# Front rows of two wide attention layers moved behind the attention steps, and another order and more gather places at the end of the last expert layer

## What is computed

```
x = x + tanh(g_xattn[n]) * xattn_n(layernorm(x), ctx_1024)
x = x + tanh(g_ffn[n])   * ffn_n(layernorm(x))
```

## Time and profile before

| | |
|---|---|
| median of 3 runs | 2029.77 us |
| the profiled execution | 2032.64 us, span 2030.8 us |
| PE busy | 1775.6 us, 87% of the span |
| DVE, ACT, POOL busy | 1259.3, 974.7, 528.6 us |
| granted PE clock, mean | 0.931 of full |

### The profile page before, as it was taken

One profiled execution on the slowest core, in us unless ns is written; L12 is line 12 of the kernel. 1 busy time (PEld: TensorE's weight loads), 2 busy tenths in 40 slices (PEclk: granted clock), 3 DMA queues, 4 the chain that ended last, 5 costly groups with the idle time before them and its releaser, 6 DMA issues. The chain is left out here.

```text
span 2030.8 us, 32563 instructions
## 1 busy us (share of the span) xinstructions
PE 1775.6 (87%) x11808; PEld 1449.2 (71%) x11808; DVE 1259.3 (62%) x2310; ACT 974.7 (48%) x1739; POOL 528.6 (26%) x492
## 2 busy tenths in 40 slices
PE   6998899967799995799999889989799799798886
PEld 4667799812577774799999467777477566588874
DVE  6886587536355454588887665556423688756643
ACT  4652467414686671377775243334433255416740
POOL 2221334244333232222220720000000144203333
PEclk9998899988899997699999989989799999899998
DMA  3003478310100000567674320000000100026742
GB/s 108 17 17 125 133 261 247 110 57 0 48 1 11 6 12 24 209 231 249 228 233 149 104 72 1 1 1 1 22 1 1 57 6 17 30 73 201 236 128 84
DMA packets 97140, 178.33 MB, mean 88 GB/s; under 512 B 25184, under 2 KB 61946, under 8 KB 95914
## 3 DMA queue, kind: packets, MB, share of 16 engines
q1 hardware_dynamic: 85496, 146.00, 21.5%
q0 software_dynamic: 11232, 30.69, 5.2%
q10 hardware_dynamic: 288, 0.00, 0.0%
HBM read 149.38 MB, written 27.26 MB: 87 GB/s over the span
## 5 line engine op out<-in xcount | busy, mean ns | idle before, releaser
L1667 POOL DMA_INDIRECT f_block_rows_home<-normed_x,f_token_of_sb x138 | 168.3, 1220 | 444.0 <-PE psum L1713 325.0
L1693 PE MATMUL psum<-f_block_h_sb,f_w1h_home 128*128 128x256 f32 x736 | 211.6, 287 | 30.2 <-DVE f_block_l_sb L1887 11.0
L1693 PE MATMUL psum<-f_block_l_sb,f_w1h_home 128*128 128x256 f32 x736 | 207.0, 281 | 0.0
L1693 PE MATMUL psum<-f_block_h_sb,f_w1l_home 128*128 128x256 f32 x736 | 207.0, 281 | 0.0
L2301 PE MATMUL psum<-a_xT_home,context_w 128*128 128x256 f32 x704 | 188.9, 415 | 13.8 <-PEq L122 9.7
L1703 PE MATMUL psum<-f_w2h_home,f_hidden_h_home 128*128 128x256 f32 x644 | 187.3, 291 | 1.9 <-DVE f_hidden_l_home L1887 1.0
L1703 PE MATMUL psum<-f_w2h_home,f_hidden_l_home 128*128 128x256 f32 x644 | 181.8, 282 | 0.0
L1703 PE MATMUL psum<-f_w2l_home,f_hidden_h_home 128*128 128x256 f32 x644 | 181.7, 282 | 0.0
L2301 PEld LDWEIGHTS psum<-a_xT_home,context_w 128*128 128x128 f32 x704 | 136.5, 204 | 47.5 <-issue 20.0
L1693 PEld LDWEIGHTS psum<-f_block_h_sb,f_w1h_home 128*128 128x128 f32 x736 | 141.2, 192 | 38.5 <-issue 28.6
L2466 ACT ACTIVATE a_probsT_sb<-psum 77x1024 f32<-77x1024 f32 (+1 forms) x128 | 130.6, 1020 | 74.8 <-PE psum L2353 72.1
(11 more groups left out here) (314 smaller groups left out, 3967.1 us busy)
## 6 DMA issues: line engine op xcount, KB each, us to landing
f_w_sb<-in_f_w SPq DMA_DIRECT2D x161, 512.0 KB
sorted_y<-f_result_sb SPq DMA_DIRECT2D x69, 256.0 KB
normed_x<-f_xn_all SPq DMA_DIRECT2D x24, 256.0 KB, 2.1
f_b_row_sb<-in_f_b SPq DMA_DIRECT2D x46, 128.0 KB
f_w_sb<-in_f_w SPq DMA_DIRECT2D x23, 256.0 KB
f_block_rows_home<-normed_x,f_token_of_sb POOLq DMA_INDIRECT x138
residual<-in_x SPq DMA_DIRECT2D x8, 256.0 KB, 6.3
context_w<-in_a_wk SPq DMA_DIRECT2D x2, 1024.0 KB, 5.1
```

Source lines behind the costliest of these rows:

```text
L1667: nc.gpsimd.indirect_dma_start(block_rows[b % 2][:, h, :], None, xs, bass.IndirectOffsetOnAxis(ap=column, axis=0)).then_inc(sems[f"rows_in ...
L1693: last = nc.tensor.matmul(hid_ps(q)[:, m, :], w, rhs, start=(j == 0), stop=(j == len(parts) - 1))
```

## The change

Three edits.

1. **Wide layers (1 and 2): the front comes behind.** With BEHIND = GROUPS + 2 = 34, `turn` of batch b is in step 34 + b, `route` in 35 + b, `logits_out` in 36 + b, and the steps go on to 43 (44 on DVE). In layer 1 the normalise of each batch stays where it was. In layer 2 that of batches 0 and 1 stays, and batch b = 2 ... 7 is normalised in step 32 + b. Layers 0 and 3 are as before.
2. **Layer 2, POOL:** all eight powers first, then all eight `add_row`. Before, they alternated.
3. **End of the last expert part:** 32 gather places (the other 16 in `xn_all`, which is free by then), so that no gather waits for a combine. DVE's order becomes: gates of units 0, 1, 2, shared result of the first batch, combines 0 to 2, gate 3, combines 3 to 6; gate 4, shared result, combines 7 to 10, gate 5, combines 11 to 14; gate 6, shared result, combines 15 to 18, gate 7, combines 19 to 22; shared result, combines 23 to 31.

In expert layer 0 the ring (8) and the order stay.

```diff
-    COMBINED = (1, 7) if shared == 1 else (4, 12, 20)
+    COMBINED = (1, 7) if shared == 1 else (3, 11, 19)
+    GATED_THEN = (7, 15, 23)
...
-    RING = 8 if own else 16
+    RING = 8 if own else 32 if t["last"] else 16
...
-    gathered = [w1[j // 4][:]... for j in range(RING)]
+    gathered = [w1[j // 4][:]... for j in range(min(RING, 16))]
+    gathered += [t["xn_all"][:, j, :] for j in range(RING - 16)]
...
-        combined = 0
+        combined, v0 = 0, U0 + BLOCKS * per_expert
+        if silu:
+            gated(dve, v0, v0 % 2)
+            gated(dve, v0 + 1, (v0 + 1) % 2)
         for k, b in enumerate(TAIL):
-            shared_block(b, U0 + BLOCKS * per_expert + k * shared)
+            more = silu and k + 1 < len(TAIL)
+            if more:
+                gated(dve, v0 + 2 * k + 2, (v0 + 2 * k + 2) % 2)
+            shared_result(dve, b, v0 + k * shared)
...
             combined = until
+            if more:
+                gated(dve, v0 + 2 * k + 3, (v0 + 2 * k + 3) % 2)
+                for j in range(combined, GATED_THEN[k]):
+                    combine(j)
+                combined = GATED_THEN[k]
...
-    FIRST, LAST = -Q_AHEAD, GROUPS + 6 + LAG
+    BEHIND = GROUPS + 2
+    FIRST, LAST = -Q_AHEAD, GROUPS + 6 + LAG if small else BEHIND + NBATCH + 2
+    XN_RING = None if FFN[n].get("routed") else 2
...
     def normed_at(s):
-        return output_at(s - 2 - LAG)
+        b = output_at(s - 2 - LAG)
+        if small or XN_RING is None:
+            return b
+        if b is not None and b < XN_RING:
+            return b
+        b = s - BEHIND + XN_RING
+        return b if XN_RING <= b < NBATCH else None
 
     def rows_at(s):
-        return output_at(s - 3 - LAG)
+        if small:
+            return output_at(s - 3)
+        return s - BEHIND if 0 <= s - BEHIND < NBATCH else None
 
     def logits_at(s):
-        return output_at(s - 4 - LAG)
+        if small:
+            return output_at(s - 4)
+        return rows_at(s - 1)
 
     def logits_out_at(s):
-        return output_at(s - 5 - LAG)
+        if small:
+            return output_at(s - 5)
+        return rows_at(s - 2)
...
                 for b in range(NBATCH):
                     front["power"](pool, b)
+                for b in range(NBATCH):
                     front["add_row"](pool, b)
```

More of the change, by code:

```diff
@@ L1517, in routed_experts @@
     result = [sb(f"result{s}", [P, BT, D]) for s in range(2)]
-    gathered = [w1[j // 4][:].rearrange("p c i -> p (c i)")[:, j % 4 * D:(j % 4 + 1) * D] for j in range(RING)]
+    gathered = [w1[j // 4][:].rearrange("p c i -> p (c i)")[:, j % 4 * D:(j % 4 + 1) * D] for j in range(min(RING, 16))]
+    gathered += [t["xn_all"][:, j, :] for j in range(RING - 16)]
     def rows_places(attention):
@@ L1879, in vector @@
     def vector(dve):
[L1880 to L1883, removed]
         def low(out, whole, part, sem):
```

## The result

The changed kernel takes 2011.95 us in the median of 4 runs (2007.16 to 2017.31), the kernel before 2029.71 beside it: ratio 0.9906, with 95% from 0.9879 to 0.9933. It is 17.8 us faster, half of the 35.5 that were forecast, and above the range's upper end of 2006. The profiled execution took 2017.31, 5.4 above the median (span 2015.5).

A forecast was written before the change was run, and what follows sets the result against it. PE was taken as the bound, losing time to waits for DVE's `logits_out`, half clock and reports held by gathers. Terms -42.5 - 15.5 + 12.5 + 5 + 5 = -35.5 took 2029.8 to 1994 us, range 1962 to 2006.

The forecast's parts named there:

- What bounds the kernel: Whole kernel: PE, busy 87%, loses time to waits for DVE's `logits_out`, half clock, and reports held back by gathers.
- Part 1: Steps of layer 2: without the front, batches lose its PE work, the waits and the half clock; 42.5 us less.
- Part 2: Steps of layer 1: batches fall from 32.1 to 28.9 us without the front; 15.5 us less in all.
- Part 3: Behind layer 2's last output: eight fronts in a row take 20 us instead of 7.4; cost 12.5 us.
- The circle: Behind layer 2's steps: `turn`, normalise, `logits_out` and `route` free one another in turn, 2.7 us a batch.
- Part 4: Behind layer 1's last output: routes held until the last batch's variance, then six follow; cost taken as 5 us.
- Part 5: End of the last layer: new order saves time, but 32 unbroken gathers delay PE's reports; 5 us more.
- the hold: Last expert part: a long unbroken row of gathers keeps PE's reports back until some 3.7 us behind its end.
- A: Rival, last layer's end: gathers don't delay PE's reports, so the end gains 23 us; 1966 us, chance 0.30.
- B: Rival, behind layers 1 and 2: fronts at half clock take 36 and 27 us; 2019 us, chance 0.06.
- C: Rival, steps of layers 1 and 2: PE's wait for the bank stays, so slower; 2047 us, chance 0.04.

The follow-up runs named there:

- rows_late: Changed kernel with POOL's `add_row` of batches 2 to 7 in layer 2 begun only when batch 5 is normalised: 2013.40 us (0.9914).
- best: Changed kernel with `logits_out` before normalise, six `add_row` late, layer 1's last variance behind four `logits_out`, POOL waiting for PE every fourth gather: 1978.64 us (0.9749).
- end_only: Kernel before with only the last layer's end changed (32 places, gates ahead of combines): 2039.68 us (1.0029).
- plain_halves: Changed kernel with 64 plain half-row transfers from POOL replacing the last layer's 32 gathers: 1974.55 us beside 2008.49; rerun 1970.01 beside 2009.4.
- last1: Changed kernel with `logits_out` before normalise in layers 1 and 2, and the last batch's variance and normalise later in layer 1: 1999.81 us (0.9848).
- after: First profile of the changed kernel itself: profiled execution 2017.31 us, where the median was 2011.95.
- again: Changed kernel itself, run again for a second profile: 2017.72 us (0.9925).

## Why the prediction was wrong, by its steps

**What bounds the kernel** was read rightly. With layer 2's front gone from the steps, wait and half clock are gone with it.

**Part 1** (-42.5): -41.7. Right, including its cycle of 26.0 us (26.2). (33.9 - 26.0 is 7.9 and not 7.8, and the three terms named for it add to 7.5; neither matters.)

**Part 2** (-15.5): -11.9 and -16.4 in the two profiles, -12.5 in the mean of the 15 profiles that have this edit (186.4 us) against the five without (198.9). The cycle was right (28.8). The 3 us went to short half-clock stretches in the last two batches, of 3.4 to 17.1 us, which come and go between executions.

**Part 3** (+12.5) is the step that failed. It priced the fronts behind the last output of layer 2 at nearly full clock: 20 us from DVE's start on that output. Measured are 27.8 us (1389.60 to 1417.4 in the first profile, and the same in all 11 profiles with this edit and this order), at half clock from the first late `route` on. That is 20.4 us more than the 7.4 of before, and just outside the bound of 27 that I had worked out for half clock. As a stretch of the table it is +19.2, since the last output product is 1.2 us shorter, and +22.2 in the first profile, with up to 1.5 more behind it.

I took 20 on the ground that gaps of PE of about 1 us do no harm, because a wait of 1.6 us in layer 1 had done none. But that one came once in a batch of 32 us, and here the gap comes in every round of 3 to 4 us. `rows_late` has no longer gap than 1.1 us in its first rounds, and its clock falls in the first of them (1392.8). `best`, where the gap is gone from the first rounds, keeps the full clock up to 1391.2 and needs 18.0 us from DVE's start. The circle itself was right in its members: at half clock they add to 4.07 us a round, and 3.94 were measured; the 2.7 were for the full clock, which no late round of the changed kernel had.

The warning that `add_row` may hold a normalise was in the text and had no price: it cost 2.7 us at the place where the clock fell. The Trainium skill, "SBUF — State Buffer", section Who interferes with whom, says that a DVE instruction in a mode with two ports and a GpSimd instruction exclude each other, the second waiting for the whole of the first, and that `tensor_scalar`, which the normalise is, can enter such a mode. The trace agrees in size: a normalise takes 0.41 us alone and up to 1.38 us beside an `add_row` of 1.26 us, and the pair of 2.01 us in `rows_late` is of the same kind. No row shows which mode DVE was in.

**Part 4** (+5): +8.1. The mechanism was as foreseen (a `logits_out` behind the last variance), but all routes behind it ran at half clock, 2.45 instead of 1.6 us a batch. Its upper bound was 7.2 for that case. The sum was short too: six routes of 1.6 us from 791.2 end at 800.8, not at 799.9.

**Part 5** (+5): +3.9 and +6.4 in the profiles, +5.9 by the medians of `end_only`. Right where it was measured: the row is unbroken, and DVE is released 2.4 to 5.4 us behind its end (forecast 3.7). But it was forecast as a property of the kernel, and it isn't one: in the last two sets it did not appear. That the result's own set was one with the hold is luck, for this part.

**The rivals.** A (no hold, 1966) came true as a mechanism in the sets without the hold. There the kernel before isn't held either, so the last part gains 11 us by the medians and not the 23. The changed kernel itself didn't run in such a set; nearest to it is `plain_halves`, 1974.55 beside 2008.49. B (ends twice as long, 2019) is nearest in size: the ends were 28 and 21 us from DVE's start instead of its 36 and 27, at half clock as it says. It had 0.06, though its mechanism stood in my own bounds. C didn't happen.

**The sum.** The parts as measured give -41.7 - 12.5 + 19.2 + 8.1 + 5.9 = -21.0; the medians say -17.8 and -16.1. The other 3 to 5 us, some of it the slower start of the next part (0.3 to 1.5 us), I can't place: single runs of the changed kernel spread over 13 us in one set. Of the 17.7 us between forecast and result 7 to 10 are part 3, 3 each parts 4 and 2, 1 each parts 1 and 5, and the rest is this.

**The range.** The forecast's own bounds, all at their worst, add to 54 - 19.6 - 7 - 8 = 19.4 us of gain, so 2010. The range ended at 2006, though the bad bounds of parts 3 and 4 had one cause, half clock behind the steps, so that they would come true together.

## What to carry to other kernels

Price short rounds moved behind a loop at the half clock, all of them, unless a trace of just such rounds shows the full one. A gap that did no harm once in a batch of 32 us says nothing about the same gap in a round of 4 us. Here only the first rounds of `best` in layer 2 had the full clock, and in layer 1 even rounds of `last1` without a wait over 0.22 us lost it. Order the engine that frees the bank so that the release stands ahead of the work that waits for PE (7 us here, 10 with the later `add_row`). Where one engine's long row of gathers runs beside a chain that depends on PE's reports, let it wait for that chain now and then: a wait every fourth gather took 23 of the 29 us off the last part, in a set with the hold. A reading of one trace that names no cause should be kept as a condition of that execution, and its absence as a case of its own.

## What the runs showed of the hardware

- PE's reports can arrive up to 28 us late beside a row of GpSimd gathers 40 us long, one every 5 to 10 us, the rest 0.06 us apart behind the row (`after`). PE's own matmuls slow to one in 0.7 to 2.1 us meanwhile. In other sets the same row (40 us, 1.25 us a gather) held nothing, and the kernel before took 2008 instead of 2030 to 2034 us. Plain transfers issued by POOL (32 in 17 us) or by SP held nothing in a set with the hold.
- The same wait of 2.7 us in layer 3 was followed by 10.2 us of half clock in `after` and by none in `again`: 4 us of a single execution are chance.
- A 128x256 normalise of DVE takes 0.41 us alone and 1.35 to 1.38 beside POOL additions of 1.26 us that follow one another (`after`, 1392.5 to 1396.4).
